# Flamingo gated block on one core: the sixteen shift transfers issued by SyncE instead of ScalarE, and the third and fourth pair's events in other slots

## What is computed

```python
q = einsum('oc,bct->bot', Wq, target) + bq      # k, v likewise from source
dot = einsum('bhdt,bhds->bhts', q, k) / sqrt(HEAD_DIM)
mask = target_mask[:, :, :, None] * source_mask[:, :, None, :]
dot = mask * dot - (1.0 - mask) * NEG
amap = softmax(dot, axis=-1) * mask
out = einsum('bhts,bhds->bhdt', amap, v)

x = x + tanh(g_xattn[0]) * xattn(layernorm(x), ctx, mask, mask, ...)
h = silu(bitlinear(layernorm(x), W1));  x = x + tanh(g_ffn[0]) * bitlinear(h, W2)
```

## Time and profile before

| | us |
|---|---|
| median of 3 runs | 215.13 (215.07 to 215.82) |
| the profiled execution, its own time | 217.99 |
| its span, first to last instruction | 216.1 |
| TensorE busy (matmul) | 187.0, 87% |
| VectorE busy | 139.9, 65% |
| ScalarE busy | 114.0, 53% |
| GpSimd busy | 92.5, 43% |
| mean granted TensorE clock | 0.953 of full |

### The profile page before, as it was taken

The page is one execution under the profiler, slowest core; times in us unless marked ns, Lnnn a source line. Parts: engine busy times, 40 slices in busy tenths (PEclk is TensorE's granted clock), DMA queues, the critical chain, the costliest instruction groups (busy, mean ns, idle before and its releaser), DMA issues.

```text
span 216.1 us, 5135 instructions
## 1 busy us (share of the span) xinstructions
PE 187.0 (87%) x1998; PEld 110.2 (51%) x1998; DVE 139.9 (65%) x276; ACT 114.0 (53%) x163; POOL 92.5 (43%) x159
## 2 busy tenths in 40 slices
PE   6886589868999799889898998898989889999764
PEld 6654334434665354545554645455555445647653
DVE  3589624565778469748975896498659772705672
ACT  2334134778158755664656456645565575573231
POOL 6496917200484626700676267006700740281250
PEclk9999557999699999999999999999999999999988
DMA  4891212780000011100000113000000000000001
GB/s 129 173 342 45 63 66 46 140 210 6 0 4 10 12 36 41 26 0 5 0 13 15 46 30 77 3 27 0 5 2 27 0 5 2 27 0 24 3 2 50
DMA packets 8408, 9.24 MB, mean 43 GB/s; under 512 B 1516, under 2 KB 6828, under 8 KB 8380
## 3 DMA queue, kind: packets, MB, share of 16 engines
q1 hardware_dynamic: 7576, 8.52, 15.3%
q10 hardware_dynamic: 808, 0.40, 0.9%
HBM read 5.66 MB, written 1.05 MB: 31 GB/s over the span
## 4 chain that ended last, share of the span: by engine, by line
PE 54%; DVE 16%; ACT 12%; POOL 6%; issue 5%; DMA 4%; SPq 1%; ACTq 1%; POOLq 0%; DVEq 0%
PE ps_exp L1044 27%; ACT probs L584 8%; DVE nmx L752 7%; PE ps_pv L1060 7%; PE ps_max L1129 3%; PE ps_max L1071 3%; PE ps_exp L1106 2%; PE ps_exp L916 2%; DMA q<-negm 2%; PE ps_max L1037 2%; DMA x_sb<-in_x 2%; PE ps_exp L1119 2%; DVE hb L800 2%; PE ps_exp L914 1%; DVE hs L805 1%
## 5 line engine op out<-in xcount | busy, mean ns | idle before, releaser
L752 DVE TENSOR_REDUCE nmx<-ps_max 128x2 f32<-128x512 f32 x122 | 79.6, 708 | 35.6 <-PE ps_max L1037 35.6
L584 ACT ACTIVATE probs<-ps_exp 128x1024 f32<-128x1024 f32 x64 | 65.4, 1022 | 59.9 <-PE ps_exp L1044 59.2
L1044 PE MATMUL ps_exp<-q,k 32*128 32x256 f32 x512 | 76.4, 416 | 14.7 <-DVE nmx L752 7.7
L1037 PE MATMUL ps_max<-k,q 32*128 32x256 f32 x488 | 73.0, 418 | 2.0 <-POOL q L342 1.3
L1044 PEld LDWEIGHTS ps_exp<-q,k 32*128 32x128 f32 x512 | 48.1, 193 | 37.6 <-issue 21.5
L1037 PEld LDWEIGHTS ps_max<-k,q 32*128 32x128 f32 x488 | 43.7, 193 | 3.0 <-POOL q L342 1.8
L1060 PE MATMUL ps_pv<-probs,v_aug 128*32 128x256 f32 x512 | 41.8, 399 | 0.0
L323 POOL TENSOR_SCALAR rstd<-mv 128x1 f32<-128x1 f32 (+1 forms) x13 | 2.9, 224 | 60.5 <-DVE mv L788 56.3
L800 DVE SCALAR_TENSOR_TENSOR hb<-hb,ps_exp 128x512 f32<-128x512 f32 x14 | 9.5, 680 | 19.7 <-ACT hb L637 19.5
L1060 PEld LDWEIGHTS ps_pv<-probs,v_aug 128*32 128x32 f32 x512 | 10.2, 109 | 21.5 <-issue 21.2
L402 POOL TENSOR_TENSOR qk<-qk,mask_b 128x512 f32<-128x512 f32 (+1 forms) x8 | 9.0, 1135 | 20.9 <-ACT qk L555 20.8
(11 more groups left out here) (159 smaller groups left out, 240.3 us busy)
## 6 DMA issues: line engine op xcount, KB each, us to landing
w_nat<-in_L_ffn_W SPq DMA_DIRECT2D x8, 256.0 KB, 4.1
out<-x_sb SPq DMA_DIRECT2D x8, 128.0 KB, 1.9
c_sb<-in_ctx SPq DMA_DIRECT2D x3, 256.0 KB, 8.1
mask_b<-in_mask_Bx1x_fk SPq DMA_DIRECT2D x1, 768.0 KB, 6.3
k<-qk SPq DMA_DIRECT2D x12, 64.0 KB
q<-qk SPq DMA_DIRECT2D x12, 64.0 KB
x_sb<-in_x SPq DMA_DIRECT2D x1, 512.0 KB, 7.2
c_sb<-in_ctx ACTq DMA_DIRECT2D x2, 128.0 KB, 3.5
```

The source lines that it names most:

```text
L584: nc.scalar.activation(probs[:, s % PROBS, :], ps_exp[:, exp_at[("exp", s)] % 2, :], ACT.Exp).then_inc(S["exp_done"], 1)
L752: nc.vector.tensor_reduce(max_columns(g, hh), ps_max[:, at % VEC, :].rearrange("t (c s) -> t c s", c=DC), AX_X, ALU.max, negate=True).then ...
L1037: return nc.tensor.matmul(bank[:, c * T:(c + 1) * T], at_rows(q4, b, h)[:, c * 128:(c + 1) * 128], at_rows(k4, b, h), start=True, stop=True)
L1044: return nc.tensor.matmul(bank[:, o:o + T], at_rows(k4, b, h)[:, c * 128:(c + 1) * 128], at_rows(q4, b, h), start=True, stop=True)
```

## The change

SyncE issues the sixteen shift transfers: a new helper `send_shift` waits for ScalarE's copy (mix_out) and issues the same DMA, at the shift's place in the slot order. ScalarE copies to negm and goes on. Pair 1 keeps its table; pairs 2 and 3 get another one, and their `qk_to_rows` waits for the last scores of the pair whose buffer is reused, as `fixed` did before.

```diff
--- before.py
+++ after.py
@@ -138,7 +138,9 @@
 
 
 
-        PAIR_EVENTS = {"fixed": -10, "stats": -10, "xn": -9, "k": -8, "rows_k": -7, "q": -6, "rows_q": -5}
+
+        NEXT_PAIR_EVENTS = {"fixed": -10, "stats": -10, "xn": -9, "k": -8, "rows_k": -7, "q": -6, "rows_q": -5}
+        PAIR_EVENTS = {"stats": -11, "xn": -10, "k": -11, "rows_k": -10, "q": -7, "fixed": -7, "rows_q": -6}
 
         FIRST_EVENTS = {"first2": -7, "second": -5, "first3": -3, "rows_k": -4, "rows_q": -4, "turn_v": -2, "copy_v": -2,
                         "mrow": -2, "v": -1, "clear_qk": -2, "clear_v": 2}
@@ -159,7 +161,8 @@
 
             use = [(w, n) for n in range(2 * B) for w, at in HALF_EVENTS.items() if s == HP // 2 * n + at]
             use += [(w, 0) for w, at in FIRST_EVENTS.items() if s == at]
-            use += [(w, p) for p in range(1, PAIRS) for w, at in PAIR_EVENTS.items() if s == 16 * p - AHEAD + at]
+            use += [(w, p) for p in range(1, PAIRS) for w, at in (PAIR_EVENTS if p > 1 else NEXT_PAIR_EVENTS).items()
+                    if s == 16 * p - AHEAD + at]
             use += [("v", p) for p in range(1, PAIRS) if s == 16 * p - V_AT]
             use += [("load_w", i) for i in W_LOADS.get(s, ())]
             use += [(w[:-1], int(w[-1])) if w[-1] in "0123" else (w, 0) for w, at in W_EVENTS.items() if s == at]
@@ -246,6 +249,8 @@
                 at, o = columns(p), "qk".index(what)
                 rows = (q4, k4)[o]
                 sp.wait_ge(S["qk_ready"], 2 * p + 2 - o)
+                if p >= 2:
+                    sp.wait_ge(S["exp_full"], exp_at[("exp", 2 * HP * (p - 1) - 1)] + 1)
                 for j in range(4):
                     sp.dma_start(rows[32 * j:32 * j + HD, p % 2, :, at], qk[32 * j:32 * j + 32, o, at]).then_inc(qk_rows[p], 16)
 
@@ -279,8 +284,16 @@
                 load_ctx(p)
 
             fixed(0)
+            def send_shift(n):
+                sp.wait_ge(S["mix_out"], mix_at[("shift", n)] + 1)
+                b, u = n // 2, n % 2 * 2
+                sp.dma_start(q4[SHIFT_ROW::32, b // 2 % 2, u:u + 2, (b % 2) * T:(b % 2 + 1) * T],
+                             negm[:]).then_inc(S["shift_in"], 16)
+
             for s in range(-AHEAD, SLOTS):
                 for what, n in events(s):
+                    if what == "shift":
+                        send_shift(n)
                     if what == "fixed":
                         fixed(n)
                     if what == "rows_k":
@@ -620,10 +633,6 @@
                         if i >= 1:
                             act.wait_ge(S["shift_in"], 16 * i)
                         nc.scalar.activation(negm[:], bank[0:HP, 0:T], ACT.Copy).then_inc(S["mix_out"], 1)
-                        act.wait_ge(S["mix_out"], mix_at[("shift", i)] + 1)
-                        b, u = i // 2, i % 2 * 2
-                        act.dma_start(q4[SHIFT_ROW::32, b // 2 % 2, u:u + 2, (b % 2) * T:(b % 2 + 1) * T],
-                                      negm[:]).then_inc(S["shift_in"], 16)
                     if what == "y_turn":
                         if i >= 1:
                             act.wait_ge(S["exp_full"], exp_at[("upb", i - 1)] + 1)
```

## The result

| | before | after |
|---|---|---|
| median in this comparison, us | 215.47 (4 runs, 215.07 to 216.92) | 218.91 (4 runs, 217.99 to 219.75) |
| ratio after to before, 95% interval | | 1.012 (1.0072 to 1.0168) |
| the profiled execution, its own time | 217.99 | 219.75 |
| its span | 216.1 | 217.9 |
| mean granted TensorE clock | 0.953 | 0.961 |

The kernel is slower by 1.2%. The forecast was 215.8 us with a range up to 217.5: wrong, and the range did not hold it either.

A forecast was written before the change was run, and what follows sets the result against it. The prediction took the kernel as bound by TensorE, broken by short waits for VectorE and ScalarE. Terms 0.1 - 0.6 + 0.25 - 0.2 + 1.1 = +0.65 took the profiled 217.99 to 218.6, median 215.8 us; range 213.6 to 217.5.

The forecast's parts named there:

- Shift 0, +0.8: Slot 0: the first shift, issued by SyncE behind pair 0's rows, arrives at 24.1; +0.8 us, between 0.1 and 2.8.
- Shift 2, slot 8 late by 0.6: Slot 8 starts 0.6 us later, shift 2 following rows and one load; swallows slot 0's 0.8; bounds 0 and +2.
- The slower rival: Early shifts wait in SyncE's queue, slot 8 1.3 late, lower clock longer: 217.4 us; 0.30 together with query or key upper ends.
- Weight totals, -0.5: Slot 9: ScalarE's fourth weight sum no longer waits behind the DMA instruction, TensorE's idle goes: -0.5 us.
- Tanh's relief, -0.6: Slots 25, 41 and 49: Tanh 0.5 earlier, slot 27 starts about 0.2 earlier; -0.6 us, between 0 and -1.5.
- Keys, +0.25 and -0.2: Key projections moved to slots 30 and 14: +0.25 us for pair 3, -0.2 for pair 2.
- the wait for y: Slot 32: y_turn waits for y, quantised on GpSimd after masking the keys; slot 33 starts 0.5 us later.
- Queries, +0.55 a pair: Query projections moved to slots 18 and 34 are no longer hidden: +0.55 us a pair, +1.1 in all, between +0.2 and +2.
- The att step: Slot 34: projection stands ahead of att, so VectorE starts its division a microsecond later; part of the +0.55.
- Rows, stores, the other shifts: Earlier rows, moved statistics and normalisation, later shifts and eight stores after shift 15: cost nothing, stores hidden by 25 us.
- the "slower" side: Outcomes above 216.2 us: the slower rival, and the forecast with query or key terms at upper ends; chance 0.30.
- The faster rival: Pairs spread well: no wait for y, att's delay absorbed, more ScalarE relief; about -1.9, 213.3 us; 0.23 in full or half.

The follow-up runs named there:

- new slots alone: Changed kernel with ScalarE issuing the shifts as before, pairs 2 and 3 on the new table: 219.48 us, ratio 1.0148 to the kernel before.
- the changed kernel with the loads first: Changed kernel with all eight weight loads issued in slot 1: 217.43 us, ratio 1.004 to the kernel before.

## Why the prediction was wrong, step by step

- **Shift 0, +0.8: wrong, 0.** It was issued at 21.50, 0.43 earlier than I had it, and arrived in 1.70 us where I had 2.1; the rows ahead cost it little or nothing beside the 1.45 of the earlier trace rows. Slot 0 waits 0.48 for it, as the forecast said, and still starts at 23.24.
- **Shift 2, slot 8 late by 0.6: measured 0.86,** with a flight of 4.65 us. The size was near, by luck: with the same start slot 7 lasts 3.48 to 4.25 in eight kernels, and the reason was another. The place in the queue does not set the flight, and the load ahead only a part (5.0 us in a queue of its own, 4.3 with no load ahead); the rows ahead carry most of it, though one kernel with the same rows did not wait (new slots alone). With the rows behind it the shift's packets pass within 1.5 us. The slower rival stood on the queue's order, with the Trainium skill's "DMA: Bandwidth & Descriptors", "Queues, rings and completion order", beside it; the shifts by themselves (issued by SyncE, old slots) gave 0.9999. The rival had the sign right and the mechanism wrong in the main. Its sum is a little off too: 215.13 + 0.65 + 0.7 + 1 is 217.5.
- **Weight totals, -0.5: right,** slot 10 4.07 to 3.58. Slots 8 and 9 in this profile fall in a stretch at half clock (slot 8 3.03 where 2.06 stood), slots 11 and 12 are out of one (2.75 and 2.06, where 3.26 and 2.34 stood), and the balance at slot 13 is +0.73; the forecast had +0.1 after slot 10. What of the difference is the wait and what is the clock's own scatter from run to run, these profiles don't settle.
- **Tanh's relief, -0.6: wrong, 0; a step that failed.** Slot 26 got shorter by 0.21, as forecast, and slot 27 longer by 0.20, likewise at slots 42 and 50. What failed is "slot 27 starts about 0.2 earlier", taken as a gain that stays. Slot 27's maxima stand behind VectorE's division, and that waits for att, which TensorE starts 1.65 us into slot 26 in both kernels. VectorE is free earlier and waits there instead:

```profile
100.09 1.29 DVE L761 TENSOR_REDUCE nmx<-ps_max 128x2 f32<-128x512 f32 x2 [0.18 <-PE ps_max L1046]
101.66 0.36 DVE L783 RECIPROCAL rec<-ps_max 128x32 f32<-128x32 f32 x1 [0.28 <-PE ps_max L1080]
```

  I had read only the wait at the front.
- **Keys, +0.25 and -0.2: right where the queries stay** (+0.23 and -0.13), with each part: slot 30 2.71, slot 33 3.67, the wait for y 0.52 in slot 32. The forecast for pair 3 is worked out step by step; the -0.2 of pair 2 has no rows for most of its steps, and its nearness to -0.13 is in part luck.
- **Queries, +0.55 a pair: the step that failed with the largest share.** Slots 34 and 35 took 7.29 and slot 36 0.13 more: +1.13 in pair 3 where the term had +0.55. The att step was right in kind and worth 0.34; with the 0.13 of slot 36 (0.2 in the forecast) that is 0.47. The other 0.66 is a conflict that a busy-time view doesn't show: queries moved one slot put GpSimd's masking beside VectorE's product by the mask, and 0.19 us became 0.85. I listed each engine's own work in slot 35 and treated the engines as independent, though the kernel before has the same product at 0.45 in entry 0, beside GpSimd's weights. The ceiling of +2 for both pairs was just passed: 0.95 + 1.14 = 2.09 with the keys moved.
- **Rows, stores, the other shifts: right,** they cost nothing. The eight stores left late and nobody waited for them. For the statistics it is right only beside the moved keys: without them slot 31 lasts 0.29 longer.
- **The sum.** Forecast +0.65; the lag that stays is +2.91 us, of which the pairs are 2.19 against 1.15, the start 0.73 against 0.1, and the missing relief 0.6. With GpSimd's hold in the list, 0.66 for each pair, the sum would have been about +2 in place of +0.65, near the "slower" side, which had 0.30. The faster rival fell on its conditions: the wait for y came, and att's delay was not absorbed. VectorE had no backlog to clear by then: it stood idle 1.14 us for att (124.77).

## What to carry to other kernels

When an event moves, list for each instruction of the busy engine not only what it waits for but what VectorE and GpSimd will run beside it: a product of 0.19 us that met a masking of 1.27 us took 0.85, and that was two thirds of what slots 34 and 35 lost. A group whose maximum lies far above its median (451 against 192 ns in the kernel before) is the place to look for such a meeting. A gain in one slot counts only if the next slot's wait does not end on the same matmul. And before a transfer is moved to another queue, see whether its arrival moves with its issue at all: here six issues 4.3 us apart were waited for until times within 1.5 us of each other.

## What the runs showed of the hardware

- A VectorE product of 128 by 32 fp32 elements from SBUF took 0.85 us beside GpSimd's product of 128 by 512, and 0.45 beside GpSimd's quantisation of weights, ending 0.04 us or less after it (five other cases: 0.19). The same with a constant as second operand: 0.84 and 0.45 (0.18 otherwise). With one operand in PSUM: 0.19 in all eight.
- An 8 KB transfer inside SBUF arrived 4.0 to 5.1 us after its issue behind row transfers and beside loads, on either queue, 7.22 us when it was issued early, and 2.78 when late, with the last packets ahead of it at 45.4 in both of the last two; the shift issued at 21.50, behind the first rows, arrived in 1.70.
- Row transfers of pair 1 (64 KB each) drained at 37 to 107 GB/s behind the loads (37.5 to 44.5 us in the changed kernel with the loads first), where weight loads reached 389.
- With a shift no longer issued by ScalarE, the 0.69 and 0.70 us that the engine stood in the earlier trace rows are gone: Tanh starts 0.18 us after the end of its matmul.
